# Second attention with rows dealt four apart to the units of mixing, and token loads placed ahead of the gate weights in the last stage

## What is computed

```
x = layernorm(x + attention_0(x))        # 16 heads of 8, rope, causal softmax
x = layernorm(x + ffn_0(x))              # gated, 128 -> 512 -> 512 -> 512 -> 128
x = layernorm(x + attention_1(x))        # see below
x = layernorm(x + moe(x))                # 16 experts of 64, top 4, and one shared

attention_1:
    q, k = l2norm(x Wq), l2norm([mem_k ; x Wk])      # 16 heads of 64, 4 memory keys ahead of the 512
    dots = 10 * q k^T                                # per head
    dots = W_pre_th @ dots                           # mixed over the 16 heads, per query row and key
    dots = causal mask, then all but the 64 largest of a row masked
    attn = W_post_th @ softmax(dots)                 # mixed over the heads again
    out  = (attn v * head_scale * sigmoid(x Wg + bg)) Wo

moe:
    probs = softmax(x gate^T); the 4 largest, scaled to sum 1, weigh the experts
    out = sum_e w_e * (silu(x w1_e) * (x w3_e)) w2_e + the same of the shared expert
```

## Time and profile before

| | us |
|---|---|
| median of 3 runs (lowest, highest) | 3411.63 (3407.72, 3423.08) |
| the profiled execution | 3420.85 |
| its span in the profile | 3419.1 |
| PE busy, share of the span | 2810.0, 82% |
| DVE | 2311.3, 68% |
| ACT | 2079.5, 61% |
| POOL | 1231.4, 36% |

### The profile page before, as it was taken

One profiled execution on the slowest core, in us unless ns is written; L12 is line 12 of the kernel. 1 busy time (PEld: TensorE's weight loads), 2 busy tenths in 40 slices (PEclk: granted clock), 3 DMA queues, 4 the chain that ended last, 5 costly groups with the idle time before them and its releaser, 6 DMA issues. The chain is left out here.

```text
span 3419.1 us, 59693 instructions
## 1 busy us (share of the span) xinstructions
PE 2810.0 (82%) x18820; PEld 1699.4 (50%) x18820; DVE 2311.3 (68%) x7708; ACT 2079.5 (61%) x5425; POOL 1231.4 (36%) x3658
## 2 busy tenths in 40 slices
PE   3778888888887788888888888888888888775887
PEld 1233333333343456556556555666565565653545
DVE  3444445544412797997997997996996996984444
ACT  0245555555534687786886886886886886762221
POOL 2111101110000464665564664664654655661000
PEclk6789998988897898998998998997997997987888
DMA  3111101100100321321222222222223123222232
GB/s 88 36 32 39 27 16 35 39 22 18 46 4 11 53 39 27 53 43 32 44 41 40 40 38 45 36 36 48 37 31 53 30 32 53 34 57 57 63 73 55
DMA packets 111296, 137.15 MB, mean 40 GB/s; under 512 B 20448, under 2 KB 90592, under 8 KB 110464
## 3 DMA queue, kind: packets, MB, share of 16 engines
q1 hardware_dynamic: 110976, 133.25, 20.9%
HBM read 47.62 MB, written 13.24 MB: 18 GB/s over the span
## 5 line engine op out<-in xcount | busy, mean ns | idle before, releaser
L1237 ACT ACTIVATE junk<-xs,thr 128x420 bf16<-128x420 f32 (+12 forms) x832 | 466.3, 571 | 88.9 <-POOL thr L953 88.2
L1066 PE MATMUL pm<-mixin,pre_b 128*128 128x258 f32 (+15 forms) x1088 | 393.4, 479 | 110.3 <-ACT xs L1230 79.9
L1079 PE MATMUL pt<-wsc,attn 128*128 128x128 f32 x2560 | 388.3, 304 | 93.6 <-POOL wsc L934 60.0
L1079 PEld LDWEIGHTS pt<-wsc,attn 128*128 128x128 f32 x2560 | 345.7, 211 | 190.1 <-POOL wsc L934 104.0
L615 DVE TENSOR_REDUCE row_max<-po 128x1 f32<-128x384 f32 (+3 forms) x352 | 209.4, 636 | 285.6 <-PE po L457 284.7
L1032 PE MATMUL pa<-kT,qT 64*128 64x258 f32 (+3 forms) x1280 | 319.1, 489 | 75.7 <-ACT arena L1199 72.7
L1356 DVE MAX8 best<-left 128x8 f32<-128x420 f32 (+12 forms) x832 | 368.2, 483 | 0.0
L1199 ACT ACTIVATE arena<-pa,nrm 128x258 f32<-128x258 f32 (+3 forms) x640 | 277.3, 485 | 128.6 <-PE pa L1032 124.6
L1066 PEld LDWEIGHTS pm<-mixin,pre_b 128*128 128x128 f32 x1088 | 189.4, 214 | 241.6 <-issue 185.7
L1386 DVE SCALAR_TENSOR_TENSOR attn<-xs,bound,ex 128x420 f32<-128x420 f32 (+14 forms) x480 | 226.2, 501 | 121.2 <-issue 66.4
L1256 ACT COPY at<-pt 128x128 f32<-128x128 f32 (+3 forms) x512 | 195.0, 441 | 150.5 <-PE po L1116 86.5
(11 more groups left out here) (235 smaller groups left out, 5988.1 us busy)
## 6 DMA issues: line engine op xcount, KB each, us to landing
spread<-gates_dram SPq DMA_DIRECT2D x32, 512.0 KB, 7.8
mixin<-arena SPq DMA_DIRECT2D x32, 258.0 KB
mixin<-arena SPq DMA_DIRECT2D x32, 242.0 KB
mixin<-arena SPq DMA_DIRECT2D x32, 226.0 KB
mixin<-arena SPq DMA_DIRECT2D x32, 210.0 KB
mixin<-arena SPq DMA_DIRECT2D x32, 194.0 KB
parts_dram<-parts SPq DMA_DIRECT2D x16, 384.0 KB, 4.1
q_stack<-parts_dram SPq DMA_DIRECT2D x96, 64.0 KB
```

Of the source, the lines that this page charges most:

```text
L1066: ins = nc.tensor.matmul(bank[:, 0:jn], pre_b[:, :], mixin[:, m % MIX_SLOTS, j0:j0 + jn], start=True, stop=not last)
L1079: ins = nc.tensor.matmul(bank[:, P * k:P * k + P], attn[:, m % A_SLOTS, P * k:P * k + P], wsc[:, m % A_SLOTS], start=True, stop=True)
L1237: ins = nc.scalar.activation(junk[:, z, 0:width(n)], xs[:, m % X_SLOTS, 0:width(n)], ACT.Sign, scale=-1.0, bias=thr[:, s % LIVE, z:z + 1], ...
```

## The change

Two parts, in two phases.

In the second phase a unit takes every fourth row of a group of 32 in place of 8 neighbours: unit n % 4 = v of a group takes rows v, v + 4, ..., v + 28. The same slice (`every`) picks the partitions that the DMA reads and the columns of `at2` and `tail` that ACT writes. The masks and the tables of thresholds are built for the new rows. Since the last 4 rows of a tile now lie in four different units, the tail is made for the last two pairs of a tile and for both units of each; `tail` is 32 columns wide instead of 8.

In the third phase the token load of batch b + 2 stands ahead of `weights_to_rows(b + 1)` in SP's stream, with 4 slots in place of 3 and a wait on the batch one earlier; `gated` has 8 slots in place of 4, and in the first batch no piece is weighed before k = 7 (the first five then one after the other).

```
-        tail = sb("tail", [P, H1, R8])
+        tail = sb("tail", [P, H1, GROUP * R8])
...
+            def every(u):
+                at = GROUP * R8 * (u // GROUP)
+                return slice(at + u % GROUP, at + GROUP * R8, GROUP)
...
             def has_tail(s):
-                return SEQ[PAIR * s % SUBS] % PER_TILE == PER_TILE - PAIR
+                return SEQ[PAIR * s % SUBS] % PER_TILE >= PER_TILE - GROUP
...
-                        tile = dots[R8 * u:R8 * u + R8, SCORES_AT[t]:SCORES_AT[t] + H1 * wt].rearrange("p (g j) -> p g j", g=H1)
+                        tile = dots[every(u), SCORES_AT[t]:SCORES_AT[t] + H1 * wt].rearrange("p (g j) -> p g j", g=H1)
...
                     bank = a_bank(("tail", s))
-                    _, m, n = pair_of(s)[-1]
-                    j0 = P * (n // PER_TILE + 1)
-                    nc.tensor.matmul(bank[0:MEM, 0:P], attn[:, m % A_SLOTS, j0:j0 + MEM], wsc[:, m % A_SLOTS],
-                                     start=True, stop=True).then_inc(a_full, 1)
+                    for z, m, n in pair_of(s):
+                        j0 = P * (n // PER_TILE + 1)
+                        ins = nc.tensor.matmul(bank[0:MEM, P * z:P * z + P], attn[:, m % A_SLOTS, j0:j0 + MEM], wsc[:, m % A_SLOTS],
+                                               start=True, stop=True)
+                    ins.then_inc(a_full, 1)
...
-                                ins = nc.tensor.matmul(bank[at:at + HD1, col + RB - R8:col + RB], vx[:, t + 1, HD1 * h:HD1 * h + HD1],
+                                ins = nc.tensor.matmul(bank[at:at + HD1, col + RB - GROUP * R8:col + RB], vx[:, t + 1, HD1 * h:HD1 * h + HD1],
...
-                        nc.scalar.copy(at2[:, 0:t + 1, :, R8 * u:R8 * u + R8],
+                        nc.scalar.copy(at2[:, 0:t + 1, :, every(u)],
...
-                        nc.scalar.copy(tail[0:MEM, :, :], bank[0:MEM, 0:P].rearrange("p (h i) -> p h i", h=H1)).then_inc(a_free, 1)
+                        for z, m, n in pair_of(s):
+                            ins = nc.scalar.copy(tail[0:MEM, :, every(n % GROUP)],
+                                                 bank[0:MEM, P * z:P * z + P].rearrange("p (h i) -> p h i", h=H1))
+                        ins.then_inc(a_free, 1)
...
-        X3 = 3
+        X3 = 4
...
-        silu1, gated = sb("silu1", [P, 2, S]), sb("gated", [P, 4, S])
+        silu1, gated = sb("silu1", [P, 2, S]), sb("gated", [P, MC, S])
...
+        WEIGHED_AFTER = {}
+        for i in range(MC * B):
+            WEIGHED_AFTER.setdefault(min(max(i + LAG, MC - 1), MC * B), []).append(i)
...
-                weights_to_rows(0)
                 for b in range(B):
+                    if b + 2 < B:
+                        if b >= 2:
+                            sp.wait_ge(y_free, b - 1)
+                        sp.dma_start(x3[:, (b + 2) % X3], x3_d[b + 2].rearrange("p (t d) -> p t d", t=TT)).then_inc(x3_in[(b + 2) % X3], 16)
+                    if b == 0:
+                        weights_to_rows(0)
                     if b + 1 < B:
                         weights_to_rows(b + 1)
-                    if b + 2 < B:
-                        if b:
-                            sp.wait_ge(y_free, b)
-                        sp.dma_start(x3[:, (b + 2) % X3], x3_d[b + 2].rearrange("p (t d) -> p t d", t=TT)).then_inc(x3_in[(b + 2) % X3], 16)
...
-                        if k < MC and MC * b + k >= LAG:
-                            weigh(MC * b + k - LAG)
+                        if k < MC:
+                            for i in WEIGHED_AFTER.get(MC * b + k, []):
+                                weigh(i)
...
-    mix = [np.where(np.arange(GROUP * R8)[None, :] > R8 * v + q[:, None] // H1, UNSEEN, 0.0) for v in range(GROUP)]
+    mix = [np.where(np.arange(GROUP * R8)[None, :] > GROUP * (q[:, None] // H1) + v, UNSEEN, 0.0) for v in range(GROUP)]
...
-            seen = R8 * n + q // H1 + 1 + MEM
+            seen = GROUP * R8 * (n // GROUP) + GROUP * (q // H1) + n % GROUP + 1 + MEM
```

More of the change, by code:

```diff
@@ L1778, in weigh @@
                     dve.wait_ge(o_free, O.nth(("m3", b, k)))
-                    nc.vector.tensor_tensor(acts[:, b % 2, k], spread[:, b % 2, k], gated[:, i % 4], ALU.mult).then_inc(weighed, 1)
+                    nc.vector.tensor_tensor(acts[:, b % 2, k], spread[:, b % 2, k], gated[:, k], ALU.mult).then_inc(weighed, 1)
                 def residual(b):
@@ L1809, in _ @@
                         dve.wait_ge(a_free, A.nth(("m1", b, k)))
-                        if k < MC and MC * b + k >= 4:
-                            dve.wait_ge(weighed, MC * b + k - 3)
-                        dst = gated[:, (MC * b + k) % 4] if k < MC else acts[0:n, b % 2, k]
+                        if k < MC and b:
+                            dve.wait_ge(weighed, MC * (b - 1) + k + 1)
+                        dst = gated[:, k] if k < MC else acts[0:n, b % 2, k]
                         nc.vector.tensor_tensor(dst, bank[0:n, :], silu1[0:n, i % 2], ALU.mult).then_inc(o_free, 1)
-                        if k < MC and MC * b + k >= LAG:
-                            weigh(MC * b + k - LAG)
+                        if k < MC:
+                            for i in WEIGHED_AFTER.get(MC * b + k, []):
+                                weigh(i)
                         if b and k == YIELD_AFTER + 2:
@@ L1826, in _ @@
                                 spread_out(b + 1)
-                for i in range(MC * B - LAG, MC * B):
+                for i in WEIGHED_AFTER[MC * B]:
                     weigh(i)
```

## The result

| | before | with the change |
|---|---|---|
| median of the runs (lowest, highest) | 3416.74 (3407.72, 3423.08) | 3466.45 (3459.76, 3471.44) |
| runs | 4 | 4 |
| the profiled execution | 3420.85 | 3471.44 |
| its span | 3419.1 | 3469.8 |

The ratio is 1.0146, 95% interval 1.0111 to 1.0182: the kernel became about 50 us slower, and the forecast (3352, range to 3418) was wrong. The parts of the forecast don't fall together, though: the third phase did what was expected, the second went the other way.

A forecast was written before the change was run, and what follows sets the result against it. DVE was taken to set the pace mid-batch in the second phase, PE at batch ends and in the third phase. -60 - 12 + 12 + 0 = -60 from 3420.9 gave 3361, 3352 on the runs' footing; range 3328 to 3418.

The forecast's parts named there:

- third phase: Third phase: the earlier token load removes all six waits and the slow-clock stretch; -60 us, ends -66 and -44.
- unit loads: Second phase, each batch's start: faster strided loads free 1.3 us seven times and about 3 at first start; -12 us.
- tail: Second phase, batch ends: extra PE tail calls 7.4 us, ring holds 5; +12 us, ends 0 and +30.
- write with a step of 16 bytes: Second phase, ACT's 512 copies into at2 with floats 16 bytes apart: 0 us, high end 133 us of ACT.
- A period without wait and slow stretch: Third phase: a batch period once the token-load wait and low-clock stretch are gone; 27.2 us, against 37.5 in the profile.
- late next: Third phase: the spreads were the next candidate to be late, but stay covered by some 3.7 us.
- each new key of the two-bank ring can also hold PE as the old one did: Second phase, batch ends: new tail keys in the ring hold PE 0.6 us, 8 times; 5 us.
- I take 0, the row nearest in kind: Second phase, at2 copies: cost taken from a trace row with 8-float inner runs, 598 ns against 592 straight; 0 us.
- rival A: Second phase: strided at2 copies add 133 us of ACT, 40% on the path, +53, total 3405 us; chance 0.22.
- rival B: Second phase: ACT becomes the bound, all 133 us on the path, 3485 us, decided from 58% on; chance 0.08.
- those 88.2 us as room: Second phase: ACT's waits for thresholds, 88.2 us, hide the tail's 24 us of copies and take in some strided-copy time.
- over 248 us: Second phase: sign that the prediction is wrong, a batch taking over 248 us; 246 was named as the batch's length.

The follow-up runs named there:

- experiment 9: Kernel before with the changed third phase and loads of every fourth row, at2 written side by side, old tail; ratio .9745.
- 1: Kernel before with the third phase of the change alone; ratio .9818, 3340.4 us.
- experiment 2: The whole change, but ACT writes at2 and tail side by side instead of with a step; ratio .9825.
- experiment 4: The whole change, but at2 written side by side while the tail copies keep their step of 4 floats; ratio .9854.

## Why the prediction was wrong

The terms of its sum, against the differences that the runs show (ratios times 3410 us). The last term is measured with the new tail, so it holds the 60 us that write and tail cost only together:

| term | predicted | ends | measured |
|---|---|---|---|
| third phase | -60 | -66, -44 | -62 (spans: -64.3) |
| unit loads | -12 | -28.8, +12 | -25 |
| tail | +12 | 0, +30 | +27 |
| write with a step of 16 bytes | 0 | 0, +133 | +109 |
| sum | -60 | | +49 |

*The third phase was right,* in size and in mechanism. "A period without wait and slow stretch" was to be 27.2 us and is 27.15; the clock is 1.00 throughout; the spreads, "late next", stayed covered.

*The unit loads* had the right mechanism, with the size too small. That loads in mid-batch are hidden held: the steps behind the second gained nothing (experiment 9 against 1). But the exposure at a batch's start was priced by DVE's 1.32 us, and the first two steps there became 2.6 us shorter. With 2.7 us at the very first load (3.6 in place of 6.3) that is 21 of the 25 us, which are themselves uncertain.

*The tail* was mis-sized too. It cost 27 us alone, near its upper end, but with slow copies 87. The step "each new key of the two-bank ring can also hold PE as the old one did" took the copy at 0.25 us and at once; in fact it stands behind two copies of the same step, so its delay is made of their length. Copying it first took off 33 of the 60 us that the two cost only together.

*The failing step is the last term.* "I take 0, the row nearest in kind": the nearest row had a short inner run but no gap between the elements, and so said nothing on the question. The runs show 0.94 ns an element more, 135 us of ACT (330.0 - 195.0) and 109 us of the kernel. The high end, 0.82 ns more and 133 us, was nearly exact. The rule of the Trainium skill that spoke against the change ("SBUF — State Buffer", "Door 1: The DMA port swizzle") was right here; it was set aside because it has no number for an ACT write. And of that ACT time rival A put 40% on the path and rival B all of it. B's time was 3485, the measured 3466; 81% of the 135 us showed (109), well over B's point of 58%. Some of that nearness is luck: with the old tail only 50 to 71 us showed, 37 to 53%, and the rest is what write and tail cost only together, which no rival had.

*B's name, however, was wrong.* ACT did not become the bound: it is busy 80% of the middle of a batch, and still waits 50.3 us for thresholds (66.7 in experiment 2, 88.2 before):

```profile
ACT junk L1242 <- POOL thr L957: 50.3, 54, 3.1
DVE attn L1393 <- ACT ex L1251: 70.6, 14, 7.5
```

The forecast read those 88.2 us as room that would take added time in. Between experiment 2 and the change only 16 us of this room were used. Told apart by steps as above, the kernel before has 11 us of these waits in a batch, and the steps where the change makes it longer, 6, 7, 11, 12 and 24 to 28, have 1.4 of them, most in step 24: the room lay in other steps.

*Two numbers of the forecast don't come out of its own rows.* The 246 us for a batch are the length of its window; from row maxima to row maxima the batches before are 244 to 257 us long, so the sign "over 248 us" was already met by the kernel before. And the ends of the terms, -66, -28.8 and 0 below and -44, +12 and +30 above, give 3317 and 3410 on the footing of 3352, not the 3328 and 3375 named as the forecast's own range.

*Its other signs spoke clearly.* Third phase 60 us shorter: yes. Second unit mixed 4 us after its issue and not 9: 1110.60, some 4 to 5 after. Copies of 600 ns or about 1010: 1093. The batches are 259 to 270 us long, all longer than before (mean 265.1 against 249.4).

## What to carry to other kernels

ACT copied float32 from PSUM at half its rate where it wrote single floats 16 bytes apart, and two floats in each 16 bytes were enough to keep the rate: try an interleave of two before one of four. A cost for which no row exists should be forecast from the end that has a mechanism, not from a row that only looks alike. And before an engine's waits are counted as room for added work, look at where they lie: here 118 to 123 us of added ACT time cost 106 to 109 us, although ACT was busy only 63% of the span. When two parts of a change use the same engine and the same ring, price them together.

## What was not expected of the hardware

ACT's write with a step of 16 bytes: 1093 to 1108 ns for 128x512 against 598 straight, 611 with a step of 8 bytes, 613 with pairs 16 bytes apart. A 4x128 tail copy rose from 250 to 402 ns with the step alone (experiment 4), to 422 in the change.

Short ACT copies in a row overlap: eight of 128x128 took 1.44 us together, where one takes 284 ns alone; two of 128x512 took 1.08. Cutting the copies, one for each tile of keys, added only 45 us for 768 more copies, 59 ns each.

```profile
1410.12 1.44 ACT L1262 COPY at<-pt 128x128 f32<-128x128 f32 x8
```
```profile
1408.23 1.08 ACT L1261 COPY at<-pt 128x512 f32<-128x512 f32 x2
```

A load of 215 KB that reads every fourth of 32 partitions is used 3.6 us after its issue, from 8 neighbours it was 6.3.

Open: the tail-first order took 33 of the 60 us by which the tail costs more with slow copies. By the steps the rest lies behind the end of the last tile but one, where the granted clock differs most (0.76 against 0.92); whether the clock is its cause was not tried.
